# Two multi-head attentions: maxima, subtraction and exponentials in halves, and GpSimd's powers between its subtractions

## The reference

```python
q = ...  # 8 sequences, 16 heads, 256 queries, 16 channels, from the normalised x
scores = einsum('bhqd,bhkd->bhqk', q, k) / sqrt(16)     # layer 1 adds a bias per key
attn = softmax(scores, axis=-1)                          # over 77 keys, all of 16 heads
out = einsum('bhqk,bhkd->bqhd', attn, v).reshape(b, n, 256)
x = x + tanh(g) * (out @ Wo)                             # layer 3 adds the bias bp
```

## Time and profile before

| | us |
|---|---|
| runs of the kernel before | 1349.92, 1341.98, 1339.06; median 1341.98 |
| the profiled execution, its own time | 1342.16 |
| its span, first to last instruction | 1340.5 |
| TensorE products / VectorE / ScalarE / GpSimd busy in the span | 1036.2 / 800.2 / 554.9 / 578.3 |

### The profile page before, as it was taken

The page is one execution under the profiler, slowest core; times in us unless marked ns, Lnnn a source line. Parts: engine busy times, 40 slices in busy tenths (PEclk is TensorE's granted clock), DMA queues, the critical chain, the costliest instruction groups (busy, mean ns, idle before and its releaser), DMA issues. The chain is left out here.

```text
span 1340.5 us, 26537 instructions
## 1 busy us (share of the span) xinstructions
PE 1036.2 (77%) x8492; PEld 771.8 (58%) x8493; DVE 800.2 (60%) x1767; ACT 554.9 (41%) x1319; POOL 578.3 (43%) x738
## 2 busy tenths in 40 slices
PE   5778287886558999940999916799987879997998
PEld 3666167784335777730899802455555557776443
DVE  4576163443383789865555544346663648886876
ACT  2452023342124666634343315556651257773000
POOL 1473703555344777634000062546662257772000
PEclk9986588998678999855999956889998979996999
DMA  3463208883113111147777421000001000000000
GB/s 110 117 178 122 102 3 289 293 296 119 54 32 114 48 36 36 48 168 283 250 254 253 168 70 53 1 1 1 1 1 47 2 12 17 16 18 6 16 23 24
DMA packets 70682, 123.47 MB, mean 92 GB/s; under 512 B 15481, under 2 KB 41859, under 8 KB 70595
## 3 DMA queue, kind: packets, MB, share of 16 engines
q1 hardware_dynamic: 63011, 101.64, 22.8%
q0 software_dynamic: 7584, 20.72, 4.6%
HBM read 52.98 MB, written 24.64 MB: 58 GB/s over the span
## 5 line engine op out<-in xcount | busy, mean ns | idle before, releaser
L2472 PE MATMUL bank<-l0f_x_high,l_weights 128*128 128x256 bf16 x256 | 51.0, 316 | 33.4 <-issue 20.2
L2881 POOL DMA_DIRECT2D l_results<-keep x23 | 12.5, 544 | 135.6 <-DVE keep L2984 129.7
L303 ACT ACTIVATE xnT<-bank 128x256 f32<-128x256 f32 (+1 forms) x112 | 41.3, 380 | 70.1 <-PE bank L292 69.3
L3256 PE MATMUL bank<-l_weights,room 128*128 x552 | 65.1, 273 | 4.3 <-DVE room L3284 2.9
L3244 PE MATMUL bank<-room,xnT 128*128 128x128 bf16 x1104 | 67.6, 223 | 0.0
L3244 PEld LDWEIGHTS bank<-room,xnT 128*128 128x128 bf16 x1104 | 65.8, 100 | 0.3
L2304 DVE SCALAR_TENSOR_TENSOR l3f_total<-bank,l3f_share,l3f_total 128x256 f32<-128x256 f32 x112 | 54.2, 484 | 15.6 <-PE bank L2222 12.0
L1849 POOL TENSOR_TENSOR l2x_probs<-l2x_probs,l2x_inverse 128x333 f32<-128x333 f32 x64 | 49.1, 789 | 29.0 <-DVE l2x_inverse L1755 29.0
L2687 PE MATMUL bank<-room,l0r_placed 128*128 128x128 bf16 x936 | 61.3, 224 | 0.0
L3256 PEld LDWEIGHTS bank<-l_weights,room 128*128 128x128 bf16 x552 | 52.7, 98 | 12.4 <-issue 5.4
L2687 PEld LDWEIGHTS bank<-room,l0r_placed 128*128 128x128 bf16 x936 | 58.2, 101 | 0.6
(11 more groups left out here) (437 smaller groups left out, 3162.5 us busy)
## 6 DMA issues: line engine op xcount, KB each, us to landing
xnT<-l_weights SPq DMA_DIRECT2D x23, 1024.0 KB, 5.1
l0r_placed<-l_weights SPq DMA_DIRECT2D x39, 512.0 KB, 3.6
l0w_staging<-in_L_ffn_weights SPq DMA_DIRECT2D x16, 480.0 KB, 3.8
l_weights<-in_L_ffn_weights SPq DMA_DIRECT2D x16, 384.0 KB, 3.1
room<-in_L_ffn_weights SPq DMA_DIRECT2D x12, 512.0 KB
room<-l_rows SPq DMA_DIRECT2D x39, 128.0 KB, 3.2
l_results<-room POOLq DMA_DIRECT2D x39, 128.0 KB, 3.1
xnT<-in_L_ffn_weights SPq DMA_DIRECT2D x8, 512.0 KB, 7.9
```

The source lines that it names most:

```text
L303: act.activation(self.chip.xnT[:, :, span(t, P)], bank[:, 0:DIM].rearrange("p (k n) -> p k n", k=KD), ACT.Copy).then_inc(self.copied, 1)
L2472: last = pe.matmul(self.bank[:, c, branch * width:(branch + 1) * width], self.weights[w][:, at:at + P], x[:, s, k, :], start=(i == 1), sto ...
L3256: last = pe.matmul(bank[:, 2 + u, 0:DIM], h[:, u, c * P:(c + 1) * P], expert_part(split[:, w, :, :], e, KD * hidden_width + c * DIM, DIM), ...
```

## The change

Maxima, subtraction and exponentials are each made in two instructions of eight heads. TensorE waits for `probs_ready` per group instead of per tile. On VectorE the maxima of the first half stand ahead of the low parts of groups 0 and 1, those of the second half ahead of groups 2 and 3. On GpSimd the order of a tile is now: first half's subtraction for tile t + 1, powers of tile t - 2 (before: of t - 1), second half's subtraction, then the values of the batch (u = 0) or the spreading of keys (u = 1, before: u = 0), x plus bias, the low weights. Two powers are left for the end.

```diff
--- before.py
+++ after.py
@@ -964,6 +964,7 @@
                     last.then_inc(scores_ready, 1)
 
             def transpose_probs(t, u, g):
+                pe.wait_ge(probs_ready, 2 * t + g // 2 + 1)
                 wait(pe, low_copied, GROUPS * t + g - 1)
                 for h in range(GROUP):
                     at = (g * GROUP + h) * KEYS
@@ -1012,7 +1013,6 @@
                 for u in range(TPB):
                     t = TPB * b + u
                     first = is_step(t, 0)
-                    pe.wait_ge(probs_ready, t + 1)
                     for half in range(2):
                         groups = (2 * half, 2 * half + 1)
                         for g in groups:
@@ -1051,16 +1051,18 @@
                                    bias=0.0 if key_bias else bq[:, m:m + 1]).then_inc(q_ready, 1)
 
             def copy_scores(t, u, groups=range(GROUPS)):
-                wait(act, shifted, t - 1)
+                wait(act, shifted, 2 * (t - 1))
                 for g in groups:
                     act.wait_ge(scores_ready, GROUPS * t + g + 1)
                     act.activation(raw[:, u, g * width:(g + 1) * width], s_bank[g % 2][:, 0:width],
                                    ACT.Copy).then_inc(scores_copied, 1)
 
             def exponents(t, u):
-                act.wait_ge(shifted, t + 1)
-                act.activation(probs[:, u, :], probs[:, u, :], ACT.Exp,
-                               scale=HEAD ** -0.5).then_inc(probs_ready, 1)
+                for half in range(2):
+                    act.wait_ge(shifted, 2 * t + half + 1)
+                    at = span(half, 2 * width)
+                    act.activation(probs[:, u, at], probs[:, u, at], ACT.Exp,
+                                   scale=HEAD ** -0.5).then_inc(probs_ready, 1)
 
             def high_probsT(t, g):
                 act.wait_ge(probs_transposed, GROUPS * t + g + 1)
@@ -1126,10 +1128,11 @@
                     source = (o_bank if b % 2 == 0 else y_bank)[0:KEYS, 0:DIM].rearrange("p (h d) -> p h d", h=HEADS)
                     dve.tensor_copy(v1[:, b, :, 0:HEAD], source).then_inc(v_ready, 1)
 
-            def maxima(t, u):
-                wait(dve, shifted, t - 1)
-                dve.wait_ge(scores_copied, GROUPS * t + GROUPS)
-                dve.tensor_reduce(row_max[:, u, :], raw[:, u, :].rearrange("p (h k) -> p h k", h=HEADS),
+            def maxima(t, u, half):
+                wait(dve, shifted, 2 * (t - 1))
+                dve.wait_ge(scores_copied, GROUPS * t + 2 * half + 2)
+                dve.tensor_reduce(row_max[:, u, span(half, CHUNK_HEADS)],
+                                  raw[:, u, span(half, 2 * width)].rearrange("p (h k) -> p h k", h=CHUNK_HEADS),
                                   AX_X, ALU.max).then_inc(max_ready, 1)
 
             def low_probsT(t, g):
@@ -1160,7 +1163,8 @@
 
             copy_v(early)
             for u in range(TPB):
-                maxima(u, u)
+                for half in range(2):
+                    maxima(u, u, half)
             copy_v(late)
             dve.wait_ge(v_high_ready, 1)
             if len(late):
@@ -1172,11 +1176,10 @@
                 for u in range(TPB):
                     t = TPB * b + u
                     for half in range(2):
-                        groups = (2 * half, 2 * half + 1)
-                        for g in groups:
+                        if not is_step(t, 0) and (ahead >= 1 or u == 0):
+                            maxima(t + 1, 1 - u, half)
+                        for g in (2 * half, 2 * half + 1):
                             low_probsT(t, g)
-                        if half == 0 and not is_step(t, 0) and (ahead >= 1 or u == 0):
-                            maxima(t + 1, 1 - u)
                     if not is_step(b, 0):
                         norm.vector_apply(dve, t - 2, u)
                         norm.vector_apply_again(dve, t - 2, u)
@@ -1207,11 +1210,13 @@
                                        head_of[:, :].unsqueeze(2).to_broadcast([P, CHUNK_HEADS, KEYS]),
                                        ALU.mult).then_inc(k_diag_ready, 1)
 
-            def shift(t, u):
-                pool.wait_ge(max_ready, t + 1)
+            def shift(t, u, half):
+                pool.wait_ge(max_ready, 2 * t + half + 1)
                 wait(pool, probs_transposed, GROUPS * (t - 1))
-                pool.tensor_tensor(probs[:, u, :].rearrange("p (h k) -> p h k", h=HEADS),
-                                   raw[:, u, :].rearrange("p (h k) -> p h k", h=HEADS), row_max[:, u, :].unsqueeze(2).to_broadcast([P, HEADS, KEYS]),
+                at, heads = span(half, 2 * width), span(half, CHUNK_HEADS)
+                pool.tensor_tensor(probs[:, u, at].rearrange("p (h k) -> p h k", h=CHUNK_HEADS),
+                                   raw[:, u, at].rearrange("p (h k) -> p h k", h=CHUNK_HEADS),
+                                   row_max[:, u, heads].unsqueeze(2).to_broadcast([P, CHUNK_HEADS, KEYS]),
                                    ALU.subtract).then_inc(shifted, 1)
 
             def place_values(b):
@@ -1221,27 +1226,32 @@
 
             spread_keys(0, 0)
             for u in range(TPB):
-                shift(u, u)
+                for half in range(2):
+                    shift(u, u, half)
             spread_keys(1, 1)
             pool.wait_ge(v_split, 1)
 
             def batch(b, ahead):
                 for u in range(TPB):
                     t = TPB * b + u
+                    early = not is_step(t, 0) and (ahead >= 1 or u == 0)
+                    if early:
+                        shift(t + 1, 1 - u, 0)
+                    if not is_step(b, 0):
+                        norm.gpsimd(pool, t - 2, u)
+                    if early:
+                        shift(t + 1, 1 - u, 1)
                     if u == 0:
                         place_values(b)
+                    elif ahead >= 2:
+                        spread_keys(b + 2, b % 2)
                     if not key_bias:
                         pool.tensor_tensor(nth(chip.x, t), nth(chip.x, t), bo[:, :], ALU.add).then_inc(x_biased, 1)
-                    if not is_step(t, 0) and (ahead >= 1 or u == 0):
-                        shift(t + 1, 1 - u)
-                    if not is_step(t, 0):
-                        norm.gpsimd(pool, t - 1, 1 - u)
-                    if u == 0 and ahead >= 2:
-                        spread_keys(b + 2, b % 2)
                     feed.low(pool, b, u)
 
             batches(pool, batch)
-            norm.gpsimd(pool, TILES - 1, 1)
+            for u in range(TPB):
+                norm.gpsimd(pool, TILES - TPB + u, u)
 
 
 L2_HEADS, L2_HEAD = 4, 64
```

## The result

The changed kernel takes 1349.53 us (median of 20 runs, 1344.10 to 1353.98), the kernel before 1343.90 us in 20 runs beside it. The ratio is 1.0048, 95% interval 1.0035 to 1.0061: **0.5% slower**, where 8 us less had been forecast. The profiled execution has a span of 1346.8 us at a mean granted clock of 0.859, against 1340.5 and 0.867.

A forecast was written before the change was run, and what follows sets the result against it. TensorE was taken as busiest, idling before tiles in a ring of low halves, maxima, subtraction, exponential and transposition. Savings of 1 us in layer 1 and 7 in layer 3, heads and tails 0, took 1342.2 to 1334 us; range 1319 to 1350.

The forecast's parts named there:

- what is removed: Both attentions: the powers' wait for moments (2.13 us layer 1, 1.54 layer 3) goes; B becomes 8.70 and 8.24 us.
- The keys in B: Spreading of keys moved to tile B runs beside its projection, ends some 2 us before needed, and costs nothing.
- what is late next: Tile A: attention waits for the values placed last on GpSimd; A takes 9.20 us in layer 1, 7.50 in layer 3.
- A gap of 1.1 us: Layer 3, before A's attention: TensorE's idle gap leaves the clock at 1.00, nothing added; 7 us saved over six batches.
- Rival 3: Both attentions: placing comes later still, slowing every tile A, clock may fall in layer 3 too; 1342 to 1357 us, chance 0.16.
- Heads and tails: First tiles and last powers of the attentions: covered or waiting as before; 0, within 1 us either way.
- The sixth, without projection: Layer 1's sixth batch: no saving or loss counted, beside 0.2 us saved in each of five batches.
- The port: Where VectorE and GpSimd meet: only VectorE's instruction is lengthened, GpSimd's subtraction is not; forecast stands at 1334 us.
- the rule: Shared ports of VectorE and GpSimd: whichever starts first blocks the other, so GpSimd would pay too; sum toward 1348 us.

The follow-up runs named there:

- values first: Changed kernel with GpSimd's placing of the batch's values moved to the head of tile A: 1329.78 us, ratio 0.9873 to the kernel before.
- halves alone: Kernel before with maxima, subtraction and exponentials in halves, every step in its old place: 1332.24 us, ratio 0.9897.
- gap filled: Changed kernel with TensorE transposing the identity (18 times in layer 1, 10 in layer 3) while waiting for the placed values: 1337.46 us, ratio 0.9938.
- placing late alone: Kernel before with only the placing of values moved, behind the whole subtraction and the powers: 1412.18 us, ratio 1.0497.
- maxima early too: Values first in layer 3; layer 1 with halves, values placed first, early half maxima, otherwise the order of before: 1276.10 us, ratio 0.9859, another chip.

## Why the prediction was wrong

**Right: what is removed.** The 2.13 us wait of the powers is gone; B takes 8.77 us in layer 1 (8.70 forecast) and 8.33 in layer 3 (1134.72 to 1143.05; 8.24). The keys in B cost nothing, as argued.

**Right: what is late next, a little too small.** A is 9.38 and 9.72 us (9.20 forecast) in layer 1, 7.72 in layer 3 (1143.05 to 1150.77; 7.50). The gap came out at 2.58 to 3.32 us instead of 2.1, and 1.5 to 1.6 instead of 1.1. In the rows: GpSimd's low weights end 2.0 us into A (1.7 forecast), and the placing took 1.58 us instead of 1.35, so the attention starts 8.00 us into A instead of 7.45. Between like attentions ten tiles apart (446.77 to 544.89) layer 1 takes 98.1 us where before it took 99.5 (447.51 to 546.98): 1.4 us saved, 1 forecast. That part of the sum held.

**Wrong: "A gap of 1.1 us is near the present one, at which the clock stayed at 1.00, so I add nothing."** This is the step that failed most: 7 of the 8 us were to come from layer 3, and its clock term was put at nothing. From the first normalised tile to the last, layer 3 took 114.62 us (window above) against 114.00 before: 0.6 us lost instead of 7 saved. Over the six batches alone, from A to A, it is 100.6 us (1117.03 to 1217.65) against 100.5 (1111.29 to 1211.81): nothing saved. The 7.2 us that are missing there divide so. Three of the first five batches ran at the clock of 0.90, 1.5 us longer each: 4.6 us. A batch without a fall takes 16.0 us instead of 15.74: 1.6 us in six. And the six batches before took 100.5 us, not six times 16.92: 1.0 us.

That the falls come from the gap is shown by two experiments: with the same wait filled, the batches take 15.9 to 16.1 us at a clock of 1.00, and in values first, where the wait is gone, the first five take 14.9 to 15.3 us at 1.00. The last batch and the tail were low before already (0.89 and 0.80) and are so now (0.89 and 0.81); values first and the filling bring the last batch to 1.00.

Rival 3 had this pairing, the placing later and the clock falling in layer 3, with 1348 to 1357 us, and I gave it 0.16. The measured 1349.53 lies in it, but that is luck in good part. It wanted the placing 1.2 us later than my sum and a gap of 2.3 us in layer 3, with a fall in every batch. The placing came about 0.5 us later, the clock fell at a gap of 1.5 us, in three batches of five, and the rest of the loss is in heads and tails, which no rival had.

**Wrong: "Heads and tails: ... 0, within 1 us either way" and "The sixth, without projection, I leave at nothing".** In layer 1 the attention of the third tile starts 18.6 us after that of the first (15.7 before), and the one of the last tile 29.2 us after that of the fourth from the end (544.89 to 574.06; 24.6 before). That is 2.8 + 4.6 us lost; less the 1.4 us gained between and 0.7 at the two ends of the window it is the layer's 5.3 us. The tail has the longest gap, 3.32 us, and from there to the layer's end, 18.7 us, the clock is 0.50; in the kernel before it was 0.97 over the eleven microseconds from 564 to 575. Layer 3's head takes 44.1 us (1073.00 to 1117.10), 40.5 before. Ahead of its first tile's third group TensorE waits 3.06 us in one piece, and ten microseconds at the low clock stand behind it:

```profile
1094.44 1.61 PEld L971 LDWEIGHTS bank<-ident,l3x_probs 128*77 128x77 f32 x8 [3.06 <-issue]
```

```profile
1094.00:1104.00 10.00, 9.53 (x78) 7.84 (x79) 5.76 (x10) 5.52 (x12) 4.00 (x6) 0.53 0.05 15
```

The head of before had such a stretch too, behind a wait of 2.45 us, but a shorter one; from 1095 on its clock is 1.00:

```profile
1086.00:1094.00 8.00, 5.83 (x21) 4.24 (x22) 4.43 (x3) 4.72 (x7) 5.64 (x7) 0.57 0.00 0
```

In values first and halves alone the head is 42.8 and 42.5 us, with the wait of 3.06 still in values first, so some 2 of its 3.6 us seem to come with the halves and the rest with the placing (1.45 us ahead of the attention at 1115.81). In gap filled it is 41.6, for the clock stayed at 1.00 behind that wait, as said above.

**The sum redrawn.** Forecast: 1 saved in layer 1, 7 in layer 3. Measured: +5.3 and +4.2 in layer length. Of the 23 us that lie between the change and values first, filling the gap gives back about 15, by the clock, and the wait itself is worth some 8 or more. I had priced the clock at 1.6 us a batch in layer 1, where that was about right (10.34 against 8.77 us), and at zero everywhere else.

**The port.** The forecast let only VectorE pay where the two meet. In A that held nearly: VectorE's instruction at 483.51 takes 1.24 us instead of 0.40, and GpSimd's subtractions take 1.22 and 1.28 (the placing's 1.58 instead of 1.35 may belong here too). In this B it did not hold:

```profile
492.34 2.01 POOL L1217 TENSOR_TENSOR l_weights<-l_weights 128x616 f32<-128x616 f32 x1
```

```profile
492.55 0.40 DVE L235 TENSOR_SCALAR l_weights<-x_res,l_weights 128x256 f32 x1
492.87 0.40 DVE L235 TENSOR_SCALAR keep<-x_res,l_weights  x1
493.38 1.25 DVE L280 SCALAR_TENSOR_TENSOR x_res<-l_weights,gate,x_res 128x256 f32 x1
```

GpSimd's subtraction takes 2.01 instead of 1.22 us. Of VectorE's instructions beside it the two first keep their 0.40, and the third takes 1.25 us where the same one takes 0.48 at 514.71. So either engine can be the one that is lengthened. The Trainium skill's page "SBUF — State Buffer", section "SBUF: two separate sides", says that of a GpSimd instruction and one of VectorE's that needs the shared pair of ports, whichever starts first gets the pair for its whole length and blocks the other. The trace agrees that both can pay; the order can't be read from the recorded starts, for GpSimd's instruction begins 0.21 us before the first that kept its 0.40. Here it fell in B, where no one waits for GpSimd. By the rule the sum went toward 1348 us; that the time came out near it is not its doing, since the 23 us of values first come with every subtraction kept. No experiment isolates the port.

**Left open.** Which gaps drop the clock. The change's trace has 2.58 us in layer 1 with a fall behind it (467.55) and 2.66 us with none (487.57), and in layer 3 1.52 us with a fall (1150.77) and 1.59 us with none (1134.72). The wait of 3.06 us in layer 3's head was followed by 0.53; in gap filled the same wait (3.07 us, ahead of 1092.03 and so ahead of that layer's first filling) was followed by 1.00. So the length of one gap does not decide it in these traces, and no run shows what does. Whether one long wait costs more clock than short ones of the same sum is suggested by layer 3 and was not tried by itself. Nor was the placing a batch ahead, into a second buffer, tried.

## What to carry to other kernels

When a step with a consumer is moved back in an engine's order, ask for each such consumer how early it must be there; here one step of about 1.5 us, ahead of or behind 4.5 us of other work, was worth 23 us, and it belonged first. A wait that moves from many small gaps into one piece is to be priced with the clock that it may cost, in the head and the tail as well as in the steady batches, and a falling clock can be tested by filling the gap with useless products. Parts of one change can need each other (here the powers between the subtractions seem to need early maxima), so undo them in pairs before calling one of them bad.

## What the runs showed that I had not expected

- Useless transpositions in the gaps made the kernel 1.1% faster than the change and 0.6% faster than before (ratio 0.9938).
- One step of 1.35 us per batch, put behind a wait for moments, cost 5.0% (placing late alone).
- The kernel before takes 1343.9 to 1346.1 us in three sets of runs and 1293.7 us in the fourth, on another chip. There the layer before the first multi-head attention ends at 350.7 us (maxima early too) instead of 399 to 404. No run shows the cause.
